# W's six block sums made by GpSimd, A's store issued by SyncE, and W's first scale spread by a matmul

## The chip, the core and the metric

One core of a Trainium2 chip runs the whole program. The metric is the device time of one launch in microseconds, the median of several runs; the profile is of one such execution. Engines are TensorE (PE in the rows, PEld for its weight loads), VectorE (DVE), ScalarE (ACT), GpSimd (POOL) and SyncE (SP, which only issues DMAs here). An engine works through its own instruction stream in order and waits in it on semaphores.

## What is computed

```
x   = x + matmul(fq(layernorm(x), s1, z1), fq(ctx, s2, z2))     # x: 2 x 1024 x 2048, ctx: 2 x 2048 x 2048
out = x + ffn(layernorm(x))
fq(x, s, z) = (clip(round(x/s + z), 0, 255) - z) * s
ffn(x): logits = x @ W_router.T ; top 2 of 8 experts, their softmax weights normalised -> w
        h = x @ lora_A (per expert, rank 16) ; lora = sum over experts of (h * w) @ lora_B, times 2
        return x @ W_base.T + b_base + lora                        # W_base: 2048 x 2048
```

## The kernel before

Phase one is the quantised product. x stands as 16 tiles of 128 rows (t = 0 to 15), ctx as 64 units u of 128 x 1024. Four lists, `SYNC`, `VEC`, `SCA` and `POOL` (lines 220 to 230), give the order of phase one on SyncE, VectorE, ScalarE and GpSimd, written out by hand. Letters with a number are steps. On SyncE: X, A and B load tile t of x (whole, first half, second half), C loads unit u of ctx, T transposes quantised tile t by DMA, P and R spill the two halves of the finished x tile to `x1d` in HBM, Y loads such a tile back for phase two, W loads a block of W. On VectorE: L is the layernorm of tile t, E evacuates group g of PSUM (`evac`, line 901, followed by two statistics instructions). On ScalarE: U quantises tile t to bytes (`xq`), V centres the transposed tile (`xc`), K centres unit u (`cc`). On GpSimd: C quantises unit u (`quantise_ctx`, line 568). TensorE multiplies tile pairs (8, 9), (10, 11) and so on in the third quarter (b = 1, h = 0), with all 16 units of ctx for a pair before the next, and single tiles in the last quarter (b = 1, h = 1), each 32 matmuls.

The LoRA matrix A and the router are split into two fp16 parts `AHI` and `ALO` and stored to `arwd` by `astore` (lines 588 to 591), in the GpSimd list between C41 and C42. Tiles 10 and 11 of x go into memory that `AHI` uses, so that SyncE's `xload` waits for that store (`s_aw`, lines 367 and 368), and all of its list behind it.

Phase two is the feed-forward product. It runs in fp16 with each factor split in two parts (three passes), and by seven block products instead of eight (as Strassen and Winograd do), for two column halves of W. Iterations i = 0 to 7 take the first half of the columns, i = 8 to 15 the second, each with two row tiles of x. The four blocks B11, B12, B21, B22 of W are 128 x 4096 fp32 each, and four sums are made of them: T3 = B22 - B12, T2 = T3 + B11, T1 = B22 - T2, T4 = B21 - T2. `wsum` makes them for the first half, `wsum1` for the second, all on VectorE. Each of the seven operands is then split: ScalarE writes the high part (`whi`, `whi1`), VectorE the low part (`wlo`, `wlo1`), two instructions each. The split needs a scale from the largest absolute row sum of W: `wabs` and `wtotal` sum on ScalarE, `wspread` writes the 128 sums to HBM and reads them back on every partition, `wscale` takes the maximum and derives the scale.

Products P1 to P7 (`product`, line 1358) use B11, B21, T2 (P6), T1 (P5), T3 (P7), B22 (P3) and T4 (P4). Their order is P1, P2, h, P6, P5, P3, P7, P4 at i = 0 and P1, P2, P6, P7, P5, P3, P4 at i = 8. A product waits for the low part of its operand (`s_wl`) and for the read of its bank (`ev`, r1 to r7). At the first iteration of each half the operands are made while the products run; these two places are called the first seam (i = 0, about 295 to 380 us) and the second seam (the end of i = 7 and i = 8, about 694 to 776 us).

Of x, ScalarE makes normalised rows (`norms`) and high parts (`chi`), VectorE low parts (`clo`, 128 x 1024, both inputs in SBUF) and sums (`csum`). `badd` adds the bias (both inputs in SBUF), `blo` is the low part of lora_B (both in SBUF), `ev` has one input in PSUM and one in SBUF.

ScalarE's `whi(3)` (T1) waits until T1 and T4 are both made (lines 730 and 731), and `whi1(5)` (T1 of the second half) does too (lines 743 to 745). `yload` of iteration 9 waits for T2 and for the low part of T3 (lines 414 to 416).

Of the kernel before, what the change touches and what calls it, by code (L numbers as in the profile page):

```python
def build(nc, x, ctxd, sc, wt, ar, bt, bias, x1d, out):
# [27 lines left out]
    with ctx:  # L29
# [137 lines left out]
        s_wm = sem("s_wm")  # L167
        s_t = sem("s_t")
# [43 lines left out]
        def plan(*lines):  # L212
# [17 lines left out]
        POOL = plan("C0-29 F0 C30-31 H0 C32-41 A0 C42-63 P8-15 R8-10 M0 R11-15")  # L230
# [127 lines left out]
        def _(sp):  # L358
# [36 lines left out]

            def qtrans(t):
# [111 lines left out]
            for kind, i in SYNC:  # L508
                {"X": xload, "A": lambda t: xhalf(t, 0), "B": lambda t: xhalf(t, 1), "C": cload, "T": qtrans, "F": fload, "P": spill_a, "R": spill_b, "Y": yload, "W": rload}[kind](i)
# [953 lines left out]
```

## Time and profile before

| | |
|---|---|
| median of 3 runs | 1056.71 us (1055.82 to 1061.08) |
| the profiled execution | 1056.88 us, span 1054.7 us |
| TensorE matmul busy | 919.1 us (87%), 4650 instructions |
| VectorE busy | 654.4 us (62%) |
| ScalarE busy | 383.8 us (36%) |
| GpSimd busy | 149.9 us (14%) |

All times of rows are in microseconds from the start of the span. Between the span and the execution's time lie 2.2 us. A matmul row whose bracket names a wait stands behind an idle stretch of TensorE. In the page's table of slices TensorE's granted clock is full (9 tenths or more) except around 150 to 200 us, at the two seams and in a few slices between, and the DMA engines are nearly full from the start to about 275 us.

### The profile page before, as it was taken

How to read it: one execution, taken by the hardware profiler on the slowest of the kernel's cores; microseconds unless marked ns; L12 is line 12 of the kernel's file. 1: busy time of each engine (PE TensorE's matmuls, PEld its weight loads, DVE VectorE, ACT ScalarE, POOL GpSimd, SP SyncE). 2: the span in 40 equal slices, each digit the busy share in tenths (PEclk: the TensorE clock that was granted, in tenths of full speed). 3: DMA queues.
4: the chain of work that ended last, by engine and by line, in shares of the span. 5: the costliest groups of instructions: out<-in, count | busy, mean ns of one | idle time of the engine just before them, and what ended most of it. 6: DMA issues, size and time to landing. Idle time of an engine off the chain costs nothing. (4 is left out here: it accounts for less than half of the span.)

```text
span 1054.7 us, 12350 instructions
## 1 busy us (share of the span) xinstructions
PE 919.1 (87%) x4650; PEld 431.9 (41%) x4672; DVE 654.4 (62%) x1007; ACT 383.8 (36%) x343; POOL 149.9 (14%) x198
## 2 busy tenths in 40 slices
PE   0989945889946578999899999998799999999997
PEld 0334422334413243545354554543244444444443
DVE  7896778534679866354746546459957545654621
ACT  3363436761534623223332333036332331331300
POOL 2643312242010011101111110100000000000000
PEclk9999987899979788999999999998899999999999
DMA  9998979799566577999799897974479898998831
GB/s 315 299 305 314 378 271 265 228 326 363 160 182 183 111 177 201 207 169 241 174 220 214 202 258 165 217 294 145 95 201 198 222 228 216 174 240 207 165 95 40
DMA packets 294142, 228.50 MB, mean 217 GB/s; under 512 B 248816, under 2 KB 249840, under 8 KB 289856
## 3 DMA queue, kind: packets, MB, share of 16 engines
q1 hardware_dynamic: 283200, 191.05, 71.0%
q0 software_dynamic: 10880, 36.61, 10.5%
q8 instruction: 40, 0.66, 0.3%
q14 instruction: 22, 0.18, 0.1%
HBM read 131.04 MB, written 36.28 MB: 159 GB/s over the span
## 5 line engine op out<-in xcount | busy, mean ns | idle before, releaser
L1380 PE MATMUL PS<-WS,XT 128*128 128x512 f16 x2688 | 602.6, 386 | 56.9 <-DVE OQ L1162 23.0
L1380 PEld LDWEIGHTS PS<-WS,XT 128*128 128x128 f16 x2688 | 265.8, 99 | 387.2 <-issue 57.4
L1334 PE MATMUL PS<-QC,QT 128*128 128x512 bf16 x1002 | 230.9, 390 | 63.9 <-DVE QC L895 29.0
L1162 DVE SCALAR_TENSOR_TENSOR OQ<-PS,ZI,OQ 128x512 f32<-128x512 f32 x128 | 94.2, 747 | 156.5 <-PE PS L1380 78.2
L1334 PEld LDWEIGHTS PS<-QC,QT 128*128 128x128 bf16 x1024 | 101.2, 100 | 193.0 <-issue 64.1
L704 ACT ACTIVATE NX<-Yb 128x1024 f16<-128x1024 f32 x60 | 63.1, 1052 | 117.3 <-DMA XT<-NX 54.4
L1088 DVE TENSOR_TENSOR NX<-Ya,NX 128x1024 f16<-128x1024 f32 x45 | 53.8, 1220 | 83.8 <-ACT NX L704 82.6
L568 POOL TENSOR_SCALAR CU<-CS,K,S 128x1024 uint8<-128x1024 f32 x64 | 79.9, 1250 | 146.5 <-DMA CS<-ctx 129.5
L598 POOL DMA_DIRECT2D out<-OQ x64 | 34.7, 542 | 450.9 <-DVE OQ L1162 440.9
L1088 DVE TENSOR_TENSOR NX<-Yb,NX 128x1024 f16<-128x1024 f32 x60 | 73.1, 1218 | 36.1 <-ACT NX L704 36.0
L672 ACT ACTIVATE QC<-CU,K 128x1024 bf16<-128x1024 uint8 x52 | 58.2, 1141 | 55.6 <-POOL CU L568 54.7
L907 DVE SCALAR_TENSOR_TENSOR XR<-PS,K,XR 128x1024 f32<-128x1024 f32 x32 | 40.8, 1276 | 55.8 <-PE PS L1334 55.8
L704 ACT ACTIVATE NX<-Ya 128x1024 f16<-128x1024 f32 x45 | 45.7, 1044 | 59.6 <-DMA XT<-NX 49.5
L689 ACT ACTIVATE Ya<-Ya,L 128x2048 f32<-128x2048 f32 x15 | 31.4, 2093 | 92.2 <-DMA Ya<-x1d 92.1
L689 ACT ACTIVATE Yb<-Yb,L 128x2048 f32<-128x2048 f32 x15 | 31.4, 2093 | 78.9 <-DMA Yb<-x1d 78.9
L1394 PE MATMUL PS<-BW,HT 128*128 128x512 f16 x192 | 50.0, 399 | 9.2 <-issue 5.9
L1411 PEld LDWEIGHTS PS<-ARW,XT 128*128 128x128 f16 x768 | 46.1, 98 | 1.9
L1411 PE MATMUL PS<-ARW,XT 128*128 128x136 f16 x768 | 46.8, 223 | 0.0
L851 DVE BATCH_NORM_STATS2 ST<-XR 128x6 f32<-128x512 f32 x64 | 39.8, 680 | 8.6 <-DMA XR<-x 8.5
L914 DVE BATCH_NORM_STATS2 ST<-XR 128x6 f32<-128x512 f32 x64 | 41.2, 685 | 1.1
L1079 DVE TENSOR_TENSOR OQ<-OQ,BI 128x512 f32<-128x512 f32 x64 | 41.0, 683 | 0.0
L658 ACT ACTIVATE XU<-XR,LN 128x2048 uint8<-128x2048 f32 x15 | 31.3, 2086 | 24.3 <-DVE LN L864 16.0
(121 smaller groups left out, 482.7 us busy)
## 6 DMA issues: line engine op xcount, KB each, us to landing
CS<-ctx SPq DMA_DIRECT2D x64, 512.0 KB, 6.4
OQ<-x1d SPq DMA_DIRECT2D x64, 256.0 KB, 4.7
out<-OQ POOLq DMA_DIRECT2D x64, 256.0 KB, 6.6
Ya<-x1d SPq DMA_DIRECT2D x15, 1024.0 KB, 6.5
Yb<-x1d SPq DMA_DIRECT2D x15, 1024.0 KB, 8.7
XR<-x SPq DMA_DIRECT2D x9, 1024.0 KB, 7.9
x1d<-XR SPq DMA_DIRECT2D x16, 512.0 KB, 8.0
FB<-wt SPq DMA_DIRECT2D x4, 2048.0 KB, 16.8
```

Source lines behind the costliest of these rows:

```text
L568: pool.tensor_scalar(CU[u % 4][:, :], CS[u % 4][:, :], k(RV2), z2, ALU.mult, ALU.add).then_inc(s_cp, 1)
L672: act.activation(QC[h][:, kt, :], CU[u % 4][:, :], ACT.Identity, bias=k(C2N)).then_inc(s_ks, 1)
L689: act.activation(Y[e][:, :], Y[e][:, :], ACT.Identity, bias=L2[:, 0, t:t + 1], scale=L2[:, 1, t:t + 1]).then_inc(s_nm, 1)
L704: act.activation(NX[nxb(n)][:, 0, :], Y[e][:, h * HF:(h + 1) * HF], ACT.Copy).then_inc(s_hi, 1)
L914: ins = dve.bn_stats(ST2[:, t, 2 * h + q, :], XR[:, h, x_slot(t), q * CH:(q + 1) * CH])
L1079: tt(OQ[b][:, :], OQ[b][:, :], BI[:, o * CH:(o + 1) * CH], ALU.add).then_inc(s_bq, 1)
L1088: tt(NX[nxb(n)][:, 1, :], blkof(e, h), NX[nxb(n)][:, 0, :], ALU.subtract).then_inc(s_lo, 1)
L1162: stt(OQ[ob][:, :], PS[:, bank(i, b), :], ZI[:, half(i), 1:2].bitcast(F32), OQ[ob][:, :], ALU.mult, ALU.add).then_inc(s_rd, 1)
L1334: ins = pe.matmul(PS[:, 2 * (t % 4) + c, :], QT[t][:, kt, :], QC[h][:, kt, c * CH:(c + 1) * CH], start=(kt == 0), stop=(kt == KT - 1))
L1380: ins = pe.matmul(PS[:, bank(i, b), :], XT[SLOT[i, j]][:, xi, kt, :], WS[half(i)][blk][:, :, kt // 2, wi, kt % 2, :], start=(fresh and n = ...
L1394: ins = pe.matmul(PS[:, bank(i, b), :], HT[i % 2][:, e, xi, :], BW[:, o, wi, :], start=False, stop=(n == 2), skip_group_check=(b == "X" or ...
L1411: ins = pe.matmul(PS[:, 7, e * 136:(e + 1) * 136], XT[SLOT[i, j]][:, xi, kt, :], ARW[:, g[wi] + kt, :], start=(n == 0), stop=(n == 47))
```

## The change

A's store moves from the GpSimd list to the SyncE list (Q0), and that list is rearranged around it. Six of the eight sums move from VectorE to GpSimd: T1 and T4 of the first half, T3, T2, T1 and T4 of the second. The four absolute sums of W are made in a row on ScalarE ahead of `chi(0, 2)`; the total is written 128 times in bf16 (`FSB`), and a matmul with an identity matrix inside the last quarter of phase one lays all totals on every partition. T3, T2 and the scale come earlier on VectorE in the first seam.

```diff
-            "P0-1 C32 P2-3 C33 R0 P4-5 C34 R1 P6-7 C35 A8-9 C36-37 B8 C38 B9 C39 R2-3 C40-41 X10-11 C42 A12-13 T8 C43 B12-13",
-            "T9 C44 R4-5 C45 A14-15 T10 C46 B14-15 T11 C47 T12 R6-7 T13 C48-49 T14 C50 T15 C51-63 Y0 W0-3")
+            "P0-1 C32-33 R0 C34 R1 C35 A8-9 C36-37 B8 C38 B9 C39-41 R2-3 Q0 P2-3 C42-43 T8 C44 T9 C45 X10-11 C46-47 R4-5",
+            "P4-5 A12-13 T10 B12-13 T11 P6-7 C48 A14-15 R6-7 T12 B14-15 T13 C49 T14 C50 T15 C51-63 Y0 W0-3")
-            "L8-9 E12-13 L10-13 E14-15 S0 L14-15 E16-23 M1")
+            "L8-9 E12-13 L10-11 E14-15 L12-13 S0 L14-15 E16-23 M1")
-        POOL = plan("C0-29 F0 C30-31 H0 C32-41 A0 C42-63 P8-15 R8-10 M0 R11-15")
+        POOL = plan("C0-29 F0 C30-31 H0 C32-63 P8-15 R8-15")
```

```diff
+            def wsum0(blk):
+
+                f = lambda b, p: FB[b][:, 4 * p:4 * p + 4, :, :].rearrange("p a b c -> p (a b c)")
+                pool.wait_ge(s_t, 2)
+                if blk == T1:
+                    slots_free(pool, 1, 0, 1, 2, 3)
+                    for p in range(2):
+                        ins = pool.tensor_tensor(f(T1, p), f(B22, p), f(T2, p), ALU.subtract)
+                else:
+                    pool.wait_ge(s_wl, 4)
+                    pool.wait_ge(s_wa, 4)
+                    for p in range(2):
+                        ins = pool.tensor_tensor(f(T4, p), f(B21, p), f(T2, p), ALU.subtract)
+                ins.then_inc(s_t, 1)
+
+            def wsum1(blk):
...
+                        ins = pool.tensor_tensor(y, b22[:, 2048 * p:2048 * (p + 1)], y, ALU.subtract)
...
+                        ins = pool.tensor_tensor(xp, y, xp, ALU.add)
...
+                    ins = pool.tensor_tensor(b22, b22, x, ALU.subtract)
...
+                    ins = pool.tensor_tensor(x, b21, x, ALU.subtract)
+                ins.then_inc(s_t, 1)
...
+            wsum0(T1)
+            wsum0(T4)
...
+                if i == NPAIR - 1:
+                    wsum1(T3)
+                    wsum1(T2)
+                store(i, (1, 1), (0, 0), (0, 1))
+                store(i, (1, 0))
+                if i == NPAIR - 1:
+                    wsum1(T1)
+                    wsum1(T4)
```

```diff
-            wabs(0)
+            for n in range(4):
+                wabs(n)
+            wtotal()
             chi(0, 2)
-            wabs(1)
-            wabs(2)
             chi(0, 3)
-            wabs(3)
-            wtotal()
+            whi(0)
             chi(0, 4)
-            whi(0)
             whi(1)
...
+                act.activation(FSB[:, :], FS[:, 8:9].to_broadcast([128, 128]), ACT.Copy).then_inc(s_wb, 1)
...
+            def wspread():
+
+                pe.wait_ge(s_ev, 28)
+                pe.wait_ge(s_wb, 1)
+                pe.matmul(PS[:, 6, 0:128], FSB[:, :], ID[:, :], start=True, stop=True).then_inc(s_wp, 1)
...
+                    if (b, t, kt) == (1, 6, 0):
+                        wspread()
+                    if (b, t, kt) == (1, 7, 0):
+                        pe.wait_ge(s_wq, 1)
```

`wsum0` and `wsum1` stand on GpSimd, `wsum0` behind R15, and wait for what the sums waited for before: in the first half T1 and T4 are two instructions of 128 x 2048 each, in the second T3 and T2 are two each and T1 and T4 one of 128 x 4096 each. `FSB` is written on ScalarE at the end of `wtotal`, and the new `wspread` is TensorE's.

VectorE's order in the first seam becomes: E26, E27, T3, `clo(0, 2)`, S1, S3, E28, T2, `wscale(0)`, E29, `clo(0, 3)`, S2, `wlo(0)`, E30, `clo(0, 4)`, S4C, `wlo(1)`, E31, `clo(0, 5)`, `clo(0, 6)`, `wlo(2)`, r1, `wlo(3)`, where T1 stood ahead of `clo(0, 6)` and T4 ahead of `wlo(3)`. In the second seam the four calls of `wsum1` fall out of VectorE's order and nothing else in it moves. The last quarter's `wspread` reads bank 6 only after E27.

## Rows read from the trace of the kernel before

**Rows 1.** Timeline of TensorE, 140 to 195 us: start, length, idle before and its releaser.
```profile
159.50 1.01 PE L1334 MATMUL PS<-QC,QT 128*128 128x512 bf16 x2 [14.49 <-issue]
165.09 14.36 PE L1334 MATMUL PS<-QC,QT 128*128 128x512 bf16 x53 [4.58 <-ACT QT L662]
...
189.66 10.58 PE L1334 MATMUL PS<-QC,QT 128*128 128x512 bf16 x37 [3.06 <-ACT QC L672]
```

**Rows 2.** Timeline of TensorE at the two seams.
```profile
309.32 7.45 PE L1380 MATMUL PS<-WS,XT 128*128 128x512 f16 x24 [14.60 <-DVE WS L1027]
347.85 12.16 PE L1380 MATMUL PS<-WS,XT 128*128 128x512 f16 x48 [11.33 <-DVE OQ L1162]
...
730.48 17.16 PE L1380 MATMUL PS<-WS,XT 128*128 128x512 f16 x72 [3.21 <-DVE WS L1062]
755.55 13.08 PE L1380 MATMUL PS<-WS,XT 128*128 128x512 f16 x48 [7.91 <-DVE WS L1062]
```

**Rows 3.** Timeline of all engines, 118 to 143 us.
```profile
118.25 1.48 DVE L964 SCALAR_TENSOR_TENSOR ALO<-ARS,SI,AHI 128x1024 f16<-128x1024 f32 x2 [1.22 <-ACT AHI L681]
...
125.31 1.56 SPq L381 DMA_DIRECT2D CS<-ctx  x2
...
126.47 2.47 DVE L851 BATCH_NORM_STATS2 ST<-XR 128x6 f32<-128x512 f32 x4 [1.72 <-DMA XR<-x]
...
132.14 0.22 DVE L864 SCALAR_TENSOR_TENSOR LN<-LN,S 128x1 f32<-128x1 f32 x1
...
137.72 0.54 POOL L591 DMA_DIRECT2D arwd<-ALO x1
...
138.28 2.08 ACT L658 ACTIVATE XU<-XR,LN 128x2048 uint8<-128x2048 f32 x1
...
142.86 1.24 SPq L369 DMA_DIRECT2D XR<-x  x2
```

**Rows 4.** Instructions grouped by line and form: count, busy, mean ns of one.
```profile
L568 POOL TENSOR_SCALAR CU<-CS,K,S 128x1024 uint8<-128x1024 f32 x64 | 79.9, 1250 | 146.5 <-DMA CS<-ctx 129.5 <-ACT QC L672 12.3 <-DVE QC L895 3.6
L1088 DVE TENSOR_TENSOR NX<-Yb,NX 128x1024 f16<-128x1024 f32 x60 | 73.1, 1218 | 36.1 <-ACT NX L704 36.0
L1039 DVE TENSOR_TENSOR FY<-FX,FY 128x2048 f32<-128x2048 f32 x2 | 4.5, 2288 | 2.8 <-DMA FX<-wt 2.8
```

**Rows 5.** Timeline of VectorE and GpSimd, 129 to 132 us.
```profile
129.91 0.16 DVE L862 SCALAR_TENSOR_TENSOR LN<-LN 128x1 f32<-128x1 f32 x1
130.21 1.20 POOL L568 TENSOR_SCALAR CU<-CS,K,S 128x1024 uint8<-128x1024 f32 x1 [1.24 <-ACT QC L672]
130.35 1.05 DVE L862 SCALAR_TENSOR_TENSOR LN<-LN 128x1 f32<-128x1 f32 x1
```

**Rows 6.** Timeline of the first seam, 300 to 340 us.
```profile
300.57 0.28 DVE L1013 TENSOR_REDUCE FX<-WG 128x1 f32<-128x128 f32 x1 [3.54 <-DMA WG<-wmd]
...
317.86 1.28 DVE L907 SCALAR_TENSOR_TENSOR XR<-PS,K,XR 128x1024 f32<-128x1024 f32 x1
...
331.02 4.41 DVE L1004 TENSOR_TENSOR FT<-FB,FT 128x4096 f32<-128x4096 f32 x1
...
335.53 3.90 ACT L732 ACTIVATE WS<-FT,ZI 128x2048 f16<-128x2048 f32 x2 [15.72 <-DVE FT L1004]
```

**Rows 7.** Timeline of the second seam, 694 to 753 us.
```profile
694.12 3.90 ACT L750 ACTIVATE WS<-FX,ZI 128x2048 f16<-128x2048 f32 x2 [14.54 <-PE PS L1380]
...
697.58 4.49 DVE L1039 TENSOR_TENSOR FY<-FX,FY 128x2048 f32<-128x2048 f32 x2 [2.79 <-DMA FX<-wt]
...
716.91 0.33 SPq L424 DMA_DIRECT2D Ya<-x1d  x1
...
725.73 4.60 DVE L1062 SCALAR_TENSOR_TENSOR WS<-FX,ZI,WS 128x2048 f16<-128x2048 f32 x2
...
730.97 3.88 ACT L750 ACTIVATE WS<-FX,ZI 128x2048 f16<-128x2048 f32 x2
...
739.79 4.42 DVE L1050 TENSOR_TENSOR FX<-FX,FX 128x4096 f32<-128x4096 f32 x1
```

More of the change, by code:

```diff
@@ L118, in build @@
         RI = small("RI", [128, 2, 8], U32)
+        ID = small("ID", [128, 128], BF16)
+        IDI = at("IDI", [128, 128], I32, R4 + 36 * KB)
         HWF = at("HWF", [128, 2, 8, 16], F32, LN_AT)
-        WG = [at("WG0", [128, 128], F32, LN_AT), at("WG1", [128, 128], F32, RB[1] + 8 * KB)]
+        FSB = at("FSB", [128, 128], BF16, LN_AT)
+        WG = at("WG", [128, 128], F32, RB[1] + 8 * KB)
         PS = ctx.enter_context(nc.psum_tensor("PS", [128, 8, CH], F32))
@@ L167, in build @@
         s_wm = sem("s_wm")
+        s_wb = sem("s_wb")
+        s_wp = sem("s_wp")
+        s_wq = sem("s_wq")
         s_t = sem("s_t")
@@ L394, in fload, with astore @@
                 sp.dma_start(BS[:, :], bt).then_inc(s_lb, 16)
+            def astore(_):
+                sp.wait_ge(s_al, 5)
+                sp.dma_start(arwd[:, 0:24, :], AHI[:, :, :]).then_inc(s_aw, 16)
+                sp.dma_start(arwd[:, 24:48, :], ALO[:, :, :]).then_inc(s_aw, 16)
             def qtrans(t):
@@ new lines, in wsum1 @@
+            def wsum1(blk):
+                x = FX1[B11][:, :, :, :].rearrange("p a b c -> p (a b c)")
+                b22, b21 = (FX1[b][:, :, :, :].rearrange("p a b c -> p (a b c)") for b in (B22, B21))
+                if blk == T3:
+                    pool.wait_ge(s_wr[0], 48)
+                    pool.wait_ge(s_wr[2], 32)
+                    for p in range(2):
+                        y = FY1[p][:, :, :, :].rearrange("p a b c -> p (a b c)")
+                        ins = pool.tensor_tensor(y, b22[:, 2048 * p:2048 * (p + 1)], y, ALU.subtract)
+                elif blk == T2:
+                    pool.wait_ge(s_t, sum1(T3))
+                    pool.wait_ge(s_wl, low1(B11, 1))
+                    for p in range(2):
+                        y = FY1[p][:, :, :, :].rearrange("p a b c -> p (a b c)")
+                        xp = x[:, 2048 * p:2048 * (p + 1)]
+                        ins = pool.tensor_tensor(xp, y, xp, ALU.add)
+                elif blk == T1:
+                    pool.wait_ge(s_t, sum1(T2))
+                    pool.wait_ge(s_wl, low1(B22, 1))
+                    ins = pool.tensor_tensor(b22, b22, x, ALU.subtract)
+                else:
+                    pool.wait_ge(s_t, sum1(T1))
+                    pool.wait_ge(s_wl, low1(T2, 1))
+                    pool.wait_ge(s_wr[3], 32)
+                    ins = pool.tensor_tensor(x, b21, x, ALU.subtract)
+                ins.then_inc(s_t, 1)
@@ L633, in _ @@
                     pool.wait_ge(s_rx, 1)
-                    wspread(1)
-                store(i, (1, 1), (0, 0), (0, 1), (1, 0))
+                    wspread()
[7 more added lines that the diff above has]
+                    wsum1(T4)
         @block.scalar
@@ L1170, in _ @@
             dve.tensor_copy(IO[:, :], IOI[:, :])
+            ts(ID[:, :], IDI[:, :], 0.0, None, ALU.is_equal)
             for kind, i in VEC:
@@ L1178, in _ @@
             evac(27)
+            wsum(T3)
             clo(0, 2)
@@ L1181, in _ @@
             csum(0, S3)
-            wsum(T3)
             evac(28)
+            wsum(T2)
+            wscale(0)
+            evac(29)
             clo(0, 3)
             csum(0, S2)
-            wsum(T2)
-            evac(29)
+            wlo(0)
+            evac(30)
             clo(0, 4)
             csum(0, S4C)
-            wscale(0)
-            wlo(0)
-            evac(30)
-            clo(0, 5)
             wlo(1)
             evac(31)
-            wsum(T1)
+            clo(0, 5)
             clo(0, 6)
@@ L1199, in _ @@
             ev(0, "r1")
-            wsum(T4)
             wlo(3)
```

74 lines of the change are left out of this document (18 added, 56 removed).

## The prediction

> **What bounds the kernel now.** I read the page's slices first: TensorE is busy 87% of the span, and its busy digit drops at the start, around 150 to 200 us and at the two seams. Then I read TensorE's own timeline for its gaps, since between them it runs matmul on matmul and only a gap can be won or lost. Around the third quarter of phase one it stands 14.5, 4.6 and 3.1 us, and once more between [rows 1]. In the first seam its two longest gaps are 14.6 us ahead of P1 and 11.3 us ahead of P5; in the second it stands 3.2 us ahead of P2 and 7.9 us ahead of P5 of iteration 8 [rows 2]. Last I followed each gap back through the other engines. After the second seam the chain that ended last is almost all matmuls, so what a seam loses is in the end time one for one.
>
> **Phase one: the store of A.** The cause of the 14.5 us is in SyncE's queue. It issues C41 by 126.9 and then nothing until 142.86, where tiles 10 and 11 wait for A's store. Both parts of A are ready at 119.7, but GpSimd issues the store's second half only at 137.7, behind C41 [rows 3]. Queued behind that wait are C42, T8, T9 and all later loads of x, and TensorE waits for them. In the change the store stands in SyncE's list behind C41 and R3, so it should go out by 127, and 4 spills of 0.5 MB each (P4 to P7) no longer stand ahead of these loads. What is late next? The layernorm of tile 8 starts at 126.5 now, waiting for x; its load comes earlier, but VectorE evacuates E10 and E11 first, so about 124.8, and 5.9 us for its steps (126.5 to 132.4 now) gives 130.7. ScalarE quantises tile 8 by 132.9 where it did so from 138.3 to 140.4 [rows 3]. T8 is then issued at 133, not 146. But tiles 10 and 11 now stand behind T8, C44, T9 and C45, and T9 waits for the quantising of tile 9 (139.5), so they are issued at about 141.6, only 1 us earlier than before. Their layernorms end at 153 and 159. From there ScalarE's order (U10 K44 U11 V10 K45 V11 U12 K46 U13 V12 K47) is a chain with a transposing DMA (about 6 us) at T10, T11 and T12, and with B12-13 issued only behind T10: I get U12 at 172, V12 at 180 and K47 at 181, where TensorE now gets K47 at 189.7 [rows 1]. I take 8 us of gain for phase one. The bounds are 1 us (all of it is lost to loads that now come later) and 14 us (the first gap gone and nothing behind it late). The third and fourth quarter run without long gaps, so the gain is passed on; the loads of W move with it, since they wait for the spills of x.
>
> **First seam.** Now the scale comes by two DMAs through HBM and VectorE reads it at 300.6 [rows 6]; P1 starts at 309.3 [rows 2]. By the matmul, with all four absolute sums made in a row, it should be known 10 us earlier, and P1 start at about 300. The matmul itself costs TensorE under 0.5 us, and the wait for the maximum ahead of tile 7 up to 1 us; both are hidden, as TensorE then waits for `wlo(0)` anyway. This gain isn't passed on, because P5 waits for T4. ScalarE's `whi(3)` waits for T1 and T4, and `wlo(3)`, `norms(1)`, `chi(1, 0)`, `clo(1, 1)` and r2 follow in a row until P5 at 347.85 [rows 2, 6]. Now T4 ends at 335.4, on VectorE [rows 6]. In the change GpSimd may start T1 only after R15, so after E31, which moves from 317.9 [rows 6] to about 309.6; that is 311.5 with the spill's issue. What a sum costs on GpSimd no row shows. The lower bound for 128 x 2048 is 2.4 us, twice its one-input instruction on 1024 columns (1.20 to 1.25 us) [rows 4, 5]; the upper is 4.8 us, if each of the two inputs takes that long. I take 4.6, twice VectorE's 2.29 for the same shape [rows 4], near the upper bound, for the next paragraph's reason. A whole sum is then 9.2 us, where VectorE takes 4.4 [rows 7].
>
> **The port.** VectorE's one-column instruction L862 takes 0.16 us; the one that began at 130.35, just behind a GpSimd instruction of 130.21 to 131.41, took 1.05 and ended with it [rows 5]. Its two inputs lie in SBUF. So an instruction of VectorE with two SBUF inputs stands until GpSimd's has ended. If the two share one read path, GpSimd can draw only one input at a time, hence twice the time for two. The low parts, `clo`, `csum`, `badd` and `blo` all have two SBUF inputs; `ev` and the evacuation have one in PSUM.
>
> The Trainium skill says the same (SBUF — State Buffer, section "Who interferes with whom"): a VectorE instruction with two SBUF inputs and a GpSimd instruction that reads SBUF exclude each other for the whole instruction. It also gives (GPSIMD Engine Reference, section "Performance versus the Vector engine") 4497 ns for this instruction on 2048 columns; no run so far shows it, and with it the sum below would be 1 us less. The rule speaks against this change: work taken from VectorE still holds it up.
>
> So in the first seam: T1's first half 311.5 to 316.1; VectorE's two `clo` (2.4) and `wlo(2)` (4.6) to 323.1; three halves of 4.6 to 336.9. T4 ends 1.5 us later than before, P5 1.3 us later: +1. Bounds: -8 (GpSimd at 2.4 per half) and +3.
>
> **Second seam.** Here VectorE loses 17.8 us of work (four sums of 4.4 to 4.5 [rows 7]), and that gains nothing, since the sums are a chain. Step by step, in the clock of the kernel before:
> - `whi1(0)`'s parts are ready at 696.1 and 698.0 [rows 7], so `wlo1(0)` takes VectorE from 696.1 to 700.8; T3, whose data lands at 697.5, waits for it on GpSimd: 700.8 to 710.0 instead of 697.6 to 702.1.
> - T2's first half 710.1 to 714.7; `wlo1(1)` (T3) stands behind it, 714.7 to 719.3; T2's second half to 723.9; three `badd` stand behind that, to 725.8; r6 and r7 to 727.2; `wlo1(2)` to 731.8; r5; `wlo1(3)` to 737.1. It ended at 730.3 [rows 7], so P2 is 6.8 us late.
> - The loads of Ya and Yb (716.9 now [rows 7]) wait for T2: 724.0. ScalarE's `norms` and `chi` end at 738.1, and `whi1(4)` starts then, where it started at 731.0 [rows 7]. `wlo1(4)` ends at 744.7, two `clo` at 747.1.
> - T1 747.1 to 756.2; `blo` 1.3; T4 757.5 to 766.6 (now both are done from 739.8 [rows 7] to 748.7).
> - `whi1(5)` and `wlo1(5)` take 6.8 us from there as they do now (748.7 to 755.5 [rows 2, 7]): P5 at 773.4 instead of 755.55, +18 us.
>
> Bounds: with GpSimd at 2.4 us per half the same steps give P5 at 756.0, so +0.5 is the lower end; at 4.8 per half they give 775.5, +20. A gain needs sums as short as VectorE's own, so I exclude one beyond 2 us. TensorE's gap ahead of L22 at i = 7 vanishes, but P5 is later than it.
>
> **Sum.** -8 + 1 + 18 = +11 us on the profiled execution's 1056.88: 1067.9. That execution is 0.2 us above the median, so 1068. Moving the store of A and spreading the scale cost nothing elsewhere; the identity matrix is made at the start, under the first load of x.
>
> **Rivals.**
> - *No lock for long instructions* (or one that VectorE always wins at once). For it: the row of the lock is of 1.2 us instructions only. Against: it held VectorE to the end of that one. Then the second seam has T3 to 706.7, T2 to 715.9, T1 and T4 737.7 to 756.1, `wlo1(5)` to 762.9: +7. In the first, T4 ends at 329.9 and P5 5 us earlier. Sum: -8 - 5 + 7 = -6, 1051: the faster side. It decides if a low part that overlaps a sum still takes 2.35 us. Chance 0.14.
> - *GpSimd is quick*, 2.4 us per half: -8 - 8 + 0.5 = -15.5, 1041. For it: its one-input rate is close to VectorE's. Against: the shared path. Chance 0.06.
> - *Phase one gives back nothing*: B12-13, A14-15 and B14-15 are behind T10, T11 and T12, and DMA is nearly full there; or the absolute sums come too late for the matmul ahead of tile 6 and TensorE stands on it. Then -1 + 1 + 18 (up to +20): 1075. Chance 0.12.
> - *A larger gain in phase one, or a milder alternation at the port*, with the mechanism as forecast: -12 + 0 + 13, about 1058. Chance 0.13.
> - The forecast: 0.55.
>
> **How the numbers follow.** The forecast's own range is 1062 to 1074. The range wanted takes in the rival without the lock and the one without the gain, and leaves out the quick GpSimd and the worst end: 1050 to 1076. About 0.5% (5 us) is what a measurement of this kernel can tell from no change. Slower by more: the forecast and phase one's rival, 0.67, less some of the forecast's low end, 0.64. Within: 0.16. Faster: 0.20.
>
> **What would show it.** Right: SyncE without its gap at 127 to 143; T8 issued near 133; TensorE's pair (8, 9) done about 8 us earlier; the first seam's P1 about 17 us earlier and its P5 about 7; GpSimd sums of 4.5 to 4.8 us per 2048 columns, more where they waited; low parts of VectorE that overlap them well over 2.35 us; a gap of 15 us or more ahead of P5 of iteration 8. Wrong: `wlo1(1)` at its old length beside T2; T1 and T4 of the second half in under 12 us together; or a gap on TensorE at tile 6 of the last quarter.

## The result, and the profile after

| | before | after |
|---|---|---|
| median, 4 runs each on one chip | 1056.26 us (1051.03 to 1061.08) | 1068.24 us (1063.56 to 1073.57) |
| ratio of the two, 95% interval | | 1.011 (1.0062 to 1.0157) |
| the profiled execution, its span | 1056.88 us, 1054.7 us | 1070.97 us, 1069.2 us |
| TensorE matmul busy | 919.1 us | 920.6 us |
| VectorE busy | 654.4 us | 667.5 us |
| GpSimd busy | 149.9 us | 207.0 us |

The change makes the kernel slower, by 12 us in the medians and 14.1 us between the two profiled executions. The total forecast, 1068.0, is met; its three terms are not all met, and this section and the experiments take them one by one. Some executions ran at a lower granted clock and took longer; among the medians of this document that moves only e1's by more than 0.5 us, since one of its four is such a one (1095.49 us at a clock of 0.904), and it is left out there.

The first thing to see in the page is that VectorE lost six sums of 4.4 us, 27 us of work, and is busy 13 us more, so its other instructions are 40 us longer. The rows of VectorE grouped by form show where most of that sits (line, operation, count, busy time, mean ns of one). The two forms of `clo` differ only in the tile they read, and both took 1.2 us before ([rows 4] has the Yb form). Of after:

```profile
L1110 DVE TENSOR_TENSOR NX<-Ya,NX 128x1024 f16<-128x1024 f32 x45 | 79.8, 1799 | 74.6 <-ACT NX L758 72.6
L1110 DVE TENSOR_TENSOR NX<-Yb,NX 128x1024 f16<-128x1024 f32 x60 | 73.1, 1219 | 40.2 <-ACT NX L758 40.1
```

A mean of 1799 ns over 45 is not 45 slower instructions. It is 43 of 1.2 us and two very long ones, of 18.6 and 9.9 us, which the seams below show. Busy time here contains waiting.

**Phase one, third quarter.** TensorE's gaps (start, length, idle before and its releaser), to set against [rows 1]:

```profile
163.49 1.04 PE L1351 MATMUL PS<-QC,QT 128*128 128x512 bf16 x4 [2.85 <-ACT QC L726]
173.24 1.89 PE L1351 MATMUL PS<-QC,QT 128*128 128x512 bf16 x4 [8.71 <-ACT QC L726]
179.90 1.89 PE L1351 MATMUL PS<-QC,QT 128*128 128x512 bf16 x4 [4.78 <-ACT QC L726]
191.26 4.02 PE L1351 MATMUL PS<-QC,QT 128*128 128x512 bf16 x9 [9.47 <-ACT QC L726]
```

The gap of 14.5 us at 159.5 is gone, and in the place of it and of the smaller ones behind it (4.6, 5.3 and 3.1 us) stand four of 2.9, 8.7, 4.8 and 9.5 us, all behind a centring on ScalarE. TensorE gets K47 at 191.3, where it got it at 189.7. The last quarter starts at 239.3 (237.8 before). The first term, a gain of 8 us, was a loss of 1.5.

**First seam**, TensorE, to set against [rows 2]:

```profile
290.65 8.77 PE L1351 MATMUL PS<-QC,QT 128*128 128x512 bf16 x31 [3.00 <-DVE FX L1059]
301.67 7.03 PE L1403 MATMUL PS<-WS,XT 128*128 128x512 f16 x24 [2.26 <-DVE WS L1077]
311.19 7.03 PE L1403 MATMUL PS<-WS,XT 128*128 128x512 f16 x24 [2.50 <-DVE WS L1077]
...
338.44 7.68 PE L1403 MATMUL PS<-WS,XT 128*128 128x512 f16 x24 [14.54 <-DVE OQ L1184]
349.28 5.96 PE L1403 MATMUL PS<-WS,XT 128*128 128x512 f16 x19 [3.16 <-DVE OQ L1184]
```

P1 starts 7.6 us earlier (301.67), P6 7.3 us later (338.44), P5 1.4 us later (349.28). What stands between is VectorE and GpSimd in the same stretch:

```profile
313.08 8.99 POOL L632 TENSOR_TENSOR FT<-FB,FT 128x2048 f32<-128x2048 f32 x2
313.48 18.58 DVE L1110 TENSOR_TENSOR NX<-Ya,NX 128x1024 f16<-128x1024 f32 x1
322.02 8.95 POOL L637 TENSOR_TENSOR FT<-FB,FT 128x2048 f32<-128x2048 f32 x2
331.98 1.21 DVE L1110 TENSOR_TENSOR NX<-Yb,NX 128x1024 f16<-128x1024 f32 x1
333.12 4.61 DVE L1077 SCALAR_TENSOR_TENSOR WS<-FT,ZI,WS 128x2048 f16<-128x2048 f32 x2
```

T1 and T4 are four instructions of 4.5 us without a pause, and one `clo` of VectorE, 1.2 us of work, is open from 313.5 to 332.1, through all four. The next `clo`, `wlo(2)` and the read r1, for which P6 waits, stand behind it.

**Second seam**, to set against [rows 7] and the last two of [rows 2]:

```profile
697.25 4.61 DVE L1084 SCALAR_TENSOR_TENSOR WS<-FX,ZI,WS 128x2048 f16<-128x2048 f32 x2 [1.37 <-ACT WS L807]
699.63 11.08 POOL L649 TENSOR_TENSOR FY<-FX,FY 128x2048 f32<-128x2048 f32 x2 [4.71 <-DMA FX<-wt]
...
712.78 11.21 DVE L1084 SCALAR_TENSOR_TENSOR WS<-FY,ZI,WS 128x2048 f16<-128x2048 f32 x2 [6.54 <-ACT WS L807]
...
737.63 18.11 PE L1403 MATMUL PS<-WS,XT 128*128 128x512 f16 x72 [14.05 <-DVE WS L1084]
...
743.67 11.01 DVE L1110 TENSOR_TENSOR NX<-Ya,NX 128x1024 f16<-128x1024 f32 x2
743.90 9.69 POOL L660 TENSOR_TENSOR FX<-FX,FX 128x4096 f32<-128x4096 f32 x1 [10.10 <-DVE WS L1084]
753.67 9.67 POOL L665 TENSOR_TENSOR FX<-FX,FX 128x4096 f32<-128x4096 f32 x1
755.26 9.16 DVE L1089 SCALAR_TENSOR_TENSOR BW<-BRAW,ZI,BW 128x1024 f16<-128x1024 f32 x1
763.43 3.89 ACT L807 ACTIVATE WS<-FX,ZI 128x2048 f16<-128x2048 f32 x2 [21.39 <-POOL FX L665]
...
770.22 5.10 PE L1403 MATMUL PS<-WS,XT 128*128 128x512 f16 x16 [14.48 <-DVE WS L1084]
```

P2 starts at 737.6 (730.5 before) and P5 at 770.2 (755.6), and the span ends 14.5 us later. P5 is 14.7 us late, of which 1.1 was there before the seam (h of iteration 7 starts at 673.7, before at 672.6): the seam costs 13.6. Here the two engines take turns. The rows of single lines (shortest, median and longest in ns, first and last start) show T2's halves and those of `wlo1(1)`:

```profile
L656 POOL TENSOR_TENSOR FX<-FY,FX x2: 4531/5549/6567, 710.8 to 715.3; 128x2048 f32<-128x2048 f32 x2
L1084 DVE SCALAR_TENSOR_TENSOR WS<-FY,ZI,WS x2: 4690/5646/6601, 712.8 to 717.4; 128x2048 f16<-128x2048 f32 x2
```

T2's first half runs from 710.8 to 715.3, and the first half of `wlo1(1)`, begun at 712.8, ends 2.2 us behind it, at 717.5. T2's second half, begun at 715.3, takes 6.6 us, 2.1 more than its own 4.5, and VectorE's second half in turn ends 2.2 us behind that. T1 and T4 of this seam are single instructions of 9.7 us; T1 began 1.0 us before the first `clo` ended, and the second `clo`, open from 744.8 to 754.7, ended 1.1 us behind T1. So each of the two sums waits about 1 us for a `clo` and takes some 8.7 us by itself; that is worked out, as no whole sum on GpSimd ran without such a turn in it.

### The profile page after: what moved, and what is told of

It is laid out like the page before. It is cut to its first block and busy times, and to the rows that moved or that the text cites. A ratio compares the mean times of both kernels' runs of the same rounds, so it can differ in the third digit from the quotient of the medians.

```text
span 1069.2 us, 12358 instructions
## 1 busy us (share of the span) xinstructions
PE 920.6 (86%) x4651; PEld 431.7 (40%) x4673; DVE 667.5 (62%) x1000; ACT 384.8 (36%) x344; POOL 207.0 (19%) x205
## 5 line engine op out<-in xcount | busy, mean ns | idle before, releaser
L1110 DVE TENSOR_TENSOR NX<-Ya,NX 128x1024 f16<-128x1024 f32 x45 | 79.8, 1799 | 74.6 <-ACT NX L758 72.6
## 6 DMA issues: line engine op xcount, KB each, us to landing
FB<-wt SPq DMA_DIRECT2D x4, 2048.0 KB, 17.5
```

Source lines behind the costliest of these rows:

```text
L1110: tt(NX[nxb(n)][:, 1, :], blkof(e, h), NX[nxb(n)][:, 0, :], ALU.subtract).then_inc(s_lo, 1)
```

## Experiments

For all of them the first number is the median, beside that of the kernel before on the same chip (1055.45 for e1 to e4, 1055.56 for e5 to e8, 1054.49 for e9 and e10), with the ratio and its 95% interval (the ratio on record, which is not exactly the quotient of the two medians). One table holds what the profiles say of the seams. "h to P5" is from the start of h at i = 7 to P5 at i = 8, so it contains the second seam and nothing that came earlier; "between" is from h at i = 1 to h at i = 7, where no experiment changed anything. Each row of it is one profiled execution.

| kernel | P1 | P5, first seam | between | h to P5 |
|---|---|---|---|---|
| before | 309.3 | 347.9 | 282.0 | 82.9 |
| after | 301.7 | 349.3 | 283.3 | 96.5 |
| e1, sums alone | 308.4 | 353.0 | 277.7 | 96.3 |
| e2, sums back | 301.3 | 342.0 | 281.1 | 81.8 |
| e3, store alone | 304.7 | 343.3 | 287.2 | 82.1 |
| e4, S0 and T12 moved | 304.0 | 351.7 | 281.2 | 96.2 |
| e5, T3 and T2 alone on GpSimd | 299.6 | 347.1 | 283.3 | 88.5 |
| e6, T1 and T4 alone on GpSimd | 301.1 | 348.8 | 279.6 | 91.2 |
| e7, other instructions | 299.8 | 330.8 | 281.2 | 86.4 |
| e8, the best parts | 294.9 | 335.3 | 280.0 | 82.2 |
| e9, low part ahead | 299.7 | 351.7 | 276.5 | 96.9 |
| e10, sums with pauses | 301.0 | 346.9 | 279.2 | 96.6 |

**e1: the kernel before, with the six sums on GpSimd and nothing else.**

```diff
 (vector, first seam)
-            wsum(T1)
             clo(0, 6)
             wlo(2)
             ev(0, "r1")
-            wsum(T4)
             wlo(3)
 (vector, second seam)
-                    wsum1(T3)
-                    wsum1(T2)
-                    wsum1(T1)
-                    wsum1(T4)
 (gpsimd, in the places of the changed kernel)
+            wsum0(T1)
+            wsum0(T4)
+                    wsum1(T3)
+                    wsum1(T2)
+                    wsum1(T1)
+                    wsum1(T4)
```

> The kernel before with only the six sums moved to GpSimd, all else as before. Theory (a sum takes GpSimd about 4.5 us per 2048 columns, and GpSimd and a VectorE instruction with two SBUF inputs exclude each other): P2 of iteration 8 about 6 us late, P5 of iteration 8 13 to 15 us late, and 0 to 3 us in the first seam, together 14 to 17 us: 1070 to 1074. Rival, that the loss comes from the rearranged first phase and not from the sums: within 3 us of the kernel before.

Measured 1072.96 us, 1.0214 (1.0148 to 1.028). The sums alone cost 17.5 us by the medians and 22.6 by the ratio, more than the whole change, so that its other parts should bring a gain (e2). P5 is 5.1 us later in the first seam (0 to 3 expected), and h to P5 is 96.3, as in the kernel after (96.5) and 13.4 over the kernel before (13 to 15 expected): 18.5 us for the two seams.

**e2: the changed kernel, with the six sums back on VectorE.**

```diff
 (vector, first seam)
             clo(0, 5)
+            wsum(T1)
             clo(0, 6)
             wlo(2)
             ev(0, "r1")
+            wsum(T4)
             wlo(3)
 (gpsimd)
-            wsum0(T1)
-            wsum0(T4)
 (second seam: T3, T2, T1, T4 likewise, in their old places)
```

> The changed kernel with its six sums back on VectorE in their old places. Theory: the second seam is as in the kernel before (gaps of about 3 and 8 us), the first seam keeps the earlier P1 (about 302) and now hands it on, P5 at 341 to 343 instead of 347.9: 1049 to 1053, 4 to 7 us under the kernel before. Rival, that the matmul for the scale and the wait on TensorE cost what they bring: 1056 to 1059.

Measured 1047.69 us, 0.9939 (0.9904 to 0.9974), 20.5 us under the kernel after and 8 us under the kernel before. The store's new list, the absolute sums in a row and the matmul together are worth 8 us, and it comes from the scale, at P1. In phase one nothing is gained:

```profile
239.71 5.52 PE L1389 MATMUL PS<-QC,QT 128*128 128x512 bf16 x17 [3.86 <-DVE XR L956]
...
301.25 7.03 PE L1441 MATMUL PS<-WS,XT 128*128 128x512 f16 x24 [3.94 <-DVE WS L1081]
```

The last quarter starts at 239.7 (237.8 before), and P1 at 301.3 (309.3). P5 is at 342.0, 7.3 us ahead of the kernel after, and h to P5 14.7 us shorter. These two, 22.0 us, are what the sums cost; the profiled executions differ by 23.9, the medians by 20.5.

**e3: the kernel before, with A's store on SyncE behind C41 and no other step moved.**

```diff
-... C40-41 X10-11 C42 A12-13 T8 ...
+... C40-41 Q0 X10-11 C42 A12-13 T8 ...
-            ... H0 C32-41 A0 C42-63 ...
+            ... H0 C32-63 ...
```

> The kernel before with only the store of A issued by SyncE, between C41 and X10-11, the lists otherwise as before. If SyncE's wait for that store (127 to 143 us) is what sets TensorE's gaps from 145 to 190, tiles 10 and 11 are asked for at about 135 to 138 and all behind them follows: pair (8, 9) ends 4 to 7 us earlier than 190.7, and the time is 1050 to 1053. Rival, that DMA is the limit there in any order: pair (8, 9) ends within 2 us of 190.7 and the time is that of the kernel before.

Measured 1054.53 us, 0.9996 (0.9965 to 1.0027): no change, where 1050 to 1053 were expected. The profile says why so little of the gap was to be had. SyncE's queue:

```profile
127.32 0.46 SPq L398 DMA_DIRECT2D arwd<-AHI  x1
127.82 0.47 SPq L399 DMA_DIRECT2D arwd<-ALO  x1
140.15 1.24 SPq L369 DMA_DIRECT2D XR<-x  x2
```

The store's second half goes out 9.9 us earlier than before (127.8, not 137.7), and the loads behind it 2.7 us earlier (140.15, not 142.86; 135 to 138 expected). Before, it landed 5.1 us after its issue; here it takes 12.3. In this kernel the DMA engines are busy for the whole stretch from 127 to 137 us (share 1.03 and 1.02 in its two halves); in the kernel before their share had fallen to 0.42 from 132 to 137, just ahead of the store. So most of SyncE's gap was never GpSimd's lateness but the time that the loads, spills and store already asked for take to land. The store also changed its queue, from GpSimd's to SyncE's, where it stands behind those transfers; how much of the 12.3 us that makes no run separates. TensorE gets K47 3 us earlier (186.8; 4 to 7 expected for the end of the pair). Its gap at 159.5 shrinks from 14.5 to 11.4 us, the last quarter starts 3.5 us earlier (234.3), P1 and P5 of the first seam are 4.6 us earlier. The end of this execution is not, since "between" took 287.2 us in it, 5.2 more than in the kernel before. In the twelve kernels of the table "between" runs from 276.5 to 287.2 with no pattern that follows their edits, so it looks like a spread from execution to execution, though with one trace of each kernel that is not shown. The ratio's interval leaves room for a gain of 0.35%, 3.7 us, at most: the 4.6 us do not all arrive at the end, and why is open.

**e4: the changed kernel, with S0 behind L14-15 on VectorE, and T12 ahead of A14-15 and R6-7 on SyncE.**

```diff
-... L10-11 E14-15 L12-13 S0 L14-15 E16-23 M1
+... L10-11 E14-15 L12-13 L14-15 S0 E16-23 M1
-... T11 P6-7 C48 A14-15 R6-7 T12 B14-15 T13 ...
+... T11 P6-7 C48 T12 A14-15 R6-7 B14-15 T13 ...
```

> The changed kernel with two steps moved in phase one: the statistics of phase two (S0) behind the layernorms of tiles 14 and 15 on VectorE, and T12 ahead of the loads A14-15 and the spills R6-7 on SyncE. If the late quantising of tile 13 (behind S0) and the late landing of T12 held K47 back in the changed kernel, K47 ends at 186 to 188 instead of 191.2 and the time falls by 3 to 4 us to about 1065. Rival, that the loads of x alone hold it: no change from 1068.

Measured 1073.51 us, 1.0186 (1.0127 to 1.0245), no gain over the kernel after (1068.24), where 1065 was expected. The local step came, and more of it than the 3 to 5 us expected, and what came next took more than it gave:

```profile
184.51 15.84 PE L1351 MATMUL PS<-QC,QT 128*128 128x512 bf16 x63 [4.91 <-ACT QC L726]
...
205.37 1.27 DVE L962 SCALAR_TENSOR_TENSOR XR<-PS,K,XR 128x1024 f32<-128x1024 f32 x1
...
206.69 1.03 PE L1351 MATMUL PS<-QC,QT 128*128 128x512 bf16 x2 [5.48 <-DVE XR L962]
```

K47 is ready at 184.5, not 191.3, and TensorE then stands 5.5 and 1.5 us on the evacuation E16, which now waits in VectorE's order for L14, L15 and S0. The last quarter starts at 241.7, later than in the kernel after (239.3). Where the order is written by hand, one step taken from a chain is a step put ahead of another.

**e5 and e6: the changed kernel with half of the second seam's sums back on VectorE.** In e5 T1 and T4 go back, in e6 T3 and T2.

```diff
 e5 (vector)
                     clo(q, 0)
                     clo(q, 1)
+                    wsum1(T1)
+                    wsum1(T4)
 e5 (gpsimd)
-                    wsum1(T1)
-                    wsum1(T4)
```

> The changed kernel with T1 and T4 of the second half back on VectorE; T3 and T2 of that half and the first half's two sums stay on GpSimd. Theory (slow and exclusive): the low part of T3 still stands beside T2, P2 of iteration 8 keeps its gap of about 14 us (6 us more than it would be late on VectorE), P5's gap falls from 14.5 to about 8; from h of iteration 7 to P5 of iteration 8 it takes 88 us, where all sums on VectorE gave 82 and all on GpSimd 96.5. Time about 1060. Rival (slow, but VectorE isn't held): T2's longer time lies beside the low part of T3 and P2 comes as with all sums on VectorE: 82 to 83 us.

> The changed kernel with T3 and T2 of the second half back on VectorE; T1 and T4 of that half and the first half's two sums stay on GpSimd. P2's gap falls back to about 3 us, T1 and T4 take 19.4 us in a row instead of 8.9, less 2.4 us of the two clo that no longer stand ahead of them: P5 8 us late, 90 us from h of iteration 7 to P5 of iteration 8. Time about 1062. The rival without the lock expects the same here, 90 to 92, since the chain is GpSimd's own; only if GpSimd were slow because VectorE holds it would this be under 86.

Measured 1058.73 us, 1.0032 (1.0004 to 1.0061), for e5 and 1063.46 us, 1.0066 (1.0036 to 1.0096), for e6. h to P5 is 88.5 in e5 and 91.2 in e6, over the 81.8 of e2: 6.7 us for T3 and T2, 9.4 us for T1 and T4, together 16.1 where both moved cost 14.7. So neither pair alone is the cause, and the rival by which VectorE isn't held (82 to 83 in e5) is out. Both kernels moved as expected (88 and 90). VectorE and TensorE in e5:

```profile
711.43 11.22 DVE L1109 SCALAR_TENSOR_TENSOR WS<-FY,ZI,WS 128x2048 f16<-128x2048 f32 x2 [6.53 <-ACT WS L804]
...
736.28 18.15 PE L1430 MATMUL PS<-WS,XT 128*128 128x512 f16 x72 [14.04 <-DVE WS L1109]
760.90 12.61 PE L1430 MATMUL PS<-WS,XT 128*128 128x512 f16 x48 [6.47 <-DVE WS L1109]
```

The 4.6 us of `wlo1(1)` took 11.2, as in the kernel after, and P5 then waits 6.5 us, about as in the kernel before (7.9). From the end of `wlo1(4)` to P5 e6 takes 26.5 us (736.2 to 762.7) and e5 17.9 (743.0 to 760.9). The 8.6 us between them are, to 0.3 us, the sums' length, 19.4 us on GpSimd with their turns in them against 8.8 on VectorE (two of 4.4, as [rows 7]), less 2.3 us for two `clo` that stand ahead of T1 on VectorE and beside it on GpSimd.

**e7: what holds the port.** The changed kernel, with the two sums of the first seam as writes without an input, and T3 and T2 of the second as instructions with one input. It leaves these four sums out, so its time is no gain; it is there for its trace.

```diff
-                        ins = pool.tensor_tensor(f(T1, p), f(B22, p), f(T2, p), ALU.subtract)
+                        ins = pool.memset(f(T1, p), 0.0)
-                        ins = pool.tensor_tensor(f(T4, p), f(B21, p), f(T2, p), ALU.subtract)
+                        ins = pool.memset(f(T4, p), 0.0)
-                        ins = pool.tensor_tensor(y, b22[...], y, ALU.subtract)
+                        ins = pool.tensor_scalar(y, b22[...], 1.0, 0.0, ALU.mult, ALU.add)
-                        ins = pool.tensor_tensor(xp, y, xp, ALU.add)
+                        ins = pool.tensor_scalar(xp, y, 1.0, 0.0, ALU.mult, ALU.add)
```

> The changed kernel with other instructions in the place of four sums on GpSimd, so that these sums are left out: T1 and T4 of the first half are memsets of the same size (they write and read nothing), T3 and T2 of the second half are one-input instructions (times 1 plus 0) of the same size. Theory (the reads exclude each other): clo(0, 5), 18.6 us in the changed kernel, takes its 1.2 us beside the memsets; the low part of T3 is still stretched by the one-input instruction beside it, though by 2.4 us at a time and not 4.5; and the one-input instruction takes 2.4 us for 2048 columns where the sum took 4.5. Rival (any GpSimd instruction excludes): clo(0, 5) is stretched beside the memsets too.

One execution, 1042.34 us. First seam, then second:

```profile
311.14 3.56 POOL L632 MEMSET FT<- 128x2048 f32 x2
311.56 1.21 DVE L1110 TENSOR_TENSOR NX<-Ya,NX 128x1024 f16<-128x1024 f32 x1
312.68 1.22 DVE L1110 TENSOR_TENSOR NX<-Yb,NX 128x1024 f16<-128x1024 f32 x1
313.82 4.61 DVE L1077 SCALAR_TENSOR_TENSOR WS<-FT,ZI,WS 128x2048 f16<-128x2048 f32 x2
...
686.45 3.76 POOL L656 TENSOR_SCALAR FX<-FY 128x2048 f32<-128x2048 f32 x2
688.44 6.17 DVE L1084 SCALAR_TENSOR_TENSOR WS<-FY,ZI,WS 128x2048 f16<-128x2048 f32 x2 [1.31 <-ACT WS L807]
```

Beside a GpSimd instruction that only writes, `clo` takes 1.21 us and `wlo(2)` 4.61, their lengths of old. Beside one that reads, VectorE is held again: the first half of `wlo1(1)`, started at 688.44, stood until T2's replacement had ended at 690.2 and ended 2.1 us later, at 692.35, so that the pair took 6.17 us and not 4.6. So it is GpSimd's reads that VectorE waits for, as far as one execution shows it. The one-input instruction takes 1.9 us per 2048 columns (3.76 for two; 2.4 expected), the two-input sum 4.5 in the other kernels. TensorE's gaps fall with them: P5 of the first seam is at 330.8, and h to P5 is 86.4, the rest being T1 and T4, which stayed.

**e8: the parts that brought a gain, together.** The sums on VectorE, the scale by the matmul, the store on SyncE, and otherwise the two lists of the kernel before.

```diff
 (against e2)
-            "P0-1 C32-33 R0 C34 R1 C35 A8-9 ... C39-41 R2-3 Q0 P2-3 C42-43 T8 C44 T9 C45 X10-11 C46-47 R4-5",
+            "P0-1 C32 P2-3 C33 R0 P4-5 C34 R1 P6-7 ... R2-3 C40-41 Q0 X10-11 C42 A12-13 T8 C43 B12-13",
-... L10-11 E14-15 L12-13 S0 ...
+... L10-13 E14-15 S0 ...
```

> All sums on VectorE, the scale by the matmul, the store of A issued by SyncE, and the lists of phase one as in the kernel before but for that store. If phase one's rearranged lists cost about 4 us against the old lists with the store moved (pair (8, 9) done at 187.7 and at 191.5), and this is handed on, the time is 1043 to 1045, under the 1047.7 of the kernel with the sums back. Rival: the stretch between the seams gives it back, 1047 to 1049.

Measured 1042.89 us, 0.9901 (0.9861 to 0.9941): 1% faster than the kernel before and 25 us faster than the one after.

TensorE's first gap of the third quarter is 11.6 us and it gets K47 at 186.3 us, much as in e3 (11.4 and 186.8), 4.3 us before e2; P1 is 6.4 us earlier than in e2, and the medians of e2 and e8 lie 4.8 us apart. So the old lists with the store moved are better than the rearranged ones, as expected. The times alone don't show it, since e3 could not be told from no change and the intervals of e2 and e8 overlap a little; with the profiles' readings of K47 and P1 it is likely.

**e9 and e10: who gets the port.** Both are the changed kernel. e9 puts the low part ahead of the two `clo`; e10 has GpSimd wait between the four sums of the first seam.

```diff
 e9 (vector)
+            wlo(2)
             clo(0, 5)
             clo(0, 6)
-            wlo(2)
 e10 (gpsimd; T4 likewise)
                         ins = pool.tensor_tensor(f(T1, p), f(B22, p), f(T2, p), ALU.subtract)
+                        if p == 0:
+                            ins.then_inc(s_gg, 1)
+                            pool.wait_ge(s_gg, 1)
...
+                    pool.wait_ge(s_t, 3)
```

> The changed kernel with wlo(2) ahead of clo(0, 5) and clo(0, 6) on VectorE; nothing else moves. In the first seam one clo stood 18.6 us through four consecutive sums of GpSimd, while in the second seam each half of wlo1(1) got the port at the end of one sum (2.3 us of its own after at most 4.4 us of waiting). Theory one: it is the kind of VectorE's instruction; the low part, with a scalar and two inputs, gets its turn between two sums where clo does not. Then the first half of wlo(2) starts at about 313.5, takes under 7 us, T1's second half is stretched to about 6.6 us, and P6 starts about 12 us earlier than 338.4. Rival: it is GpSimd's side, four sums handed over without a pause; then the first half of wlo(2) is open for about 19.7 us, to 1 to 2 us behind the end of T4, and P6 starts within 3 us of where it did.

> The changed kernel with GpSimd made to wait between the four sums of the first seam: each starts only when the semaphore of the one before has come. The wait by itself costs under 0.2 us each. Theory: VectorE gets the port where GpSimd pauses, as between T1 and T4 of the second half, where T4 waits for T1's semaphore and a clo ran for 1.1 us between them. Then clo(0, 5) ends 1.1 us behind T1's first half (about 5.2 us in all, not 18.6), T1's second half is stretched to about 5.5 us, clo(0, 6) and the two halves of wlo(2) each follow at the end of one more sum, P6 starts 6 to 10 us earlier, and T4 ends 4 to 6 us later. Rival: a pause of 0.1 us makes no difference; clo(0, 5) is open for 18 us or more again and P6 starts near 338.4.

One execution each, 1068.57 and 1066.27 us. VectorE in e9, and VectorE and GpSimd in e10:

```profile
311.48 19.65 DVE L1077 SCALAR_TENSOR_TENSOR WS<-FT,ZI,WS 128x2048 f16<-128x2048 f32 x1
```

```profile
312.37 9.98 POOL L633 TENSOR_TENSOR FT<-FB,FT 128x2048 f32<-128x2048 f32 x2
312.76 5.21 DVE L1118 TENSOR_TENSOR NX<-Ya,NX 128x1024 f16<-128x1024 f32 x1
317.90 5.54 DVE L1118 TENSOR_TENSOR NX<-Yb,NX 128x1024 f16<-128x1024 f32 x1
...
322.52 11.78 POOL L642 TENSOR_TENSOR FT<-FB,FT 128x2048 f32<-128x2048 f32 x2 [0.17 <-POOL FT L633]
323.37 13.08 DVE L1085 SCALAR_TENSOR_TENSOR WS<-FT,ZI,WS 128x2048 f16<-128x2048 f32 x2
```

(In e10 T4 also waits for T1's semaphore, `s_t` at 3, which it doesn't in the changed kernel.) In e9 the low part stands 19.65 us for its 2.3, as the rival had it: the kind of VectorE's instruction isn't what decides. In e10 `clo` is done after 5.21 us, as the theory had it, and the engines take turns from there on. That buys little, as every turn lengthens the sums: they end at 334.3, not 331.0, though they start 0.7 us earlier, the halves of `wlo(2)` take 6.6 us each, and P6 comes at 337.2 (I had 6 to 10 us earlier than 338.4), P5 at 346.9, where P2 is 0.7 us earlier too.

## Why the prediction came out as it did

The total was right, 1068.0 against 1068.24, because two errors of it cancel in part, and luck covers the rest: a gain of 8 us that did not come, and a loss set 5.5 us too high. Between the two profiled executions the sum reads: phase one +1.5, first seam -0.1 (P5 is 1.4 us late and the last quarter had been 1.5), second seam +13.6. These are 15.0; the end of the span is 14.5 us later, as 0.3 us come back between P5 and h of iteration 7 and 0.2 behind the second seam. Against the steps' -8, +1 and +18 the misses are +9.5, -1.1 and -4.4, together +4. The profiled execution is 3 us over the forecast's 1067.9, and it lies 2.7 us above its kernel's median, which is why the median agrees to less than a microsecond. That closeness is luck.

- **Phase one, -8: wrong.** The first steps held: SyncE's gap is gone, the store's halves go out at 124.9 and 126.2, tile 8 is quantised from 132.5 on and T8 issued at 134.6 (forecast 133). The step that failed is "tiles 10 and 11 are issued at about 141.6".

```profile
129.35 2.26 SPq L387 DMA_DIRECT2D CS<-ctx  x2
...
141.13 2.45 POOL L580 TENSOR_SCALAR CU<-CS,K,S 128x1024 uint8<-128x1024 f32 x2 [9.89 <-DMA CS<-ctx]
142.36 1.15 ACT L726 ACTIVATE QC<-CU,K 128x1024 bf16<-128x1024 uint8 x1 [7.79 <-POOL CU L580]
143.41 2.08 ACT L712 ACTIVATE XU<-XR,LN 128x2048 uint8<-128x2048 f32 x1
...
145.57 1.24 SPq L414 DMA_TRANSPOSE XV<-XU  x1
...
147.47 1.24 SPq L375 DMA_DIRECT2D XR<-x  x2
```

  GpSimd waits 9.9 us for C42, which was issued at 129.4 and is there only at 141.1, with the store and the spills issued just ahead of it; that these slowed it is argued from the order, not shown. ScalarE centres it (K42) ahead of U9 in its order, so tile 9 is quantised from 143.4 on and not from 137.5, T9 goes out at 145.6 (139.5 forecast), and X10-11 behind it at 147.5: 5.9 us later than forecast and 4.6 later than before. I had counted the DMAs' issues and let the landings stand as they were. The forecast also took SyncE's wait for the cause of TensorE's gap without asking how much of it was landing; e3 shows 12.3 us of it with the store issued at once.
- **The end of phase one.** A second step was left out: the last steps of L13 come behind S0 in VectorE's stream. The statistics of tile 13 end at 179.0, its aggregation follows at 183.6, and U13 starts at 186.2. K47 comes last, behind V12 and T12, which is issued at 178.9 behind the loads of A14-15 and lands at 187.1. V12 stands behind U13 in ScalarE's order and starts at 188.2 (180 forecast); U12, which stands ahead of both, started at 176.7 (172 forecast). e4 moves S0 and T12 and K47 comes 6.7 us earlier: shown for the two together, not for each. That this is no gain for the kernel, since E16 then waits, is shown too.

```profile
179.05 1.12 DVE L1025 BATCH_NORM_AGGREGATE MV<-ST 128x2 f32<-128x24 f32 x8
...
183.61 0.26 DVE L912 BATCH_NORM_AGGREGATE LN<-ST 128x2 f32<-128x24 f32 x1
```

  The rival "phase one gives back nothing" had the outcome right here. Of its causes, full DMA engines fit (their share is 0.96 to 1.15 from 124 to 141 us) but aren't shown to be the cause, and the gap on TensorE ahead of tile 6 did not come.
- **First seam, +1: right in size, wrong inside.** With the 1.5 us of phase one taken off, P1 starts at 300.2 (forecast 300) and T1 at 311.6 (311.5). The matmul cost TensorE 0.2 us. The wait for the maximum ahead of tile 7 was 3.0 us (forecast up to 1; 0.5 in e2), hidden as said, since P1 starts within 0.5 us of e2's. A half of a sum took 4.50 us, not 4.6. The step that failed is the order at the port: two `clo` and `wlo(2)` were to slip in behind T1's first half, and did not. So T4 ends at 329.5 on that clock, 7.4 us before the forecast, and `wlo(2)` starts at 331.6, 13 us behind it, and the two nearly cancel at P5 (347.8, forecast 349.1). The way to P5 is another than the forecast's too: it had T4's end, then ScalarE's `whi(3)`; in the trace `whi(3)` starts 4.5 us after T4's end, behind the first half of `wlo(2)`, and VectorE's queue follows T4's end without a gap, `clo`, `wlo(2)`, r1 and `wlo(3)`, from 332.0 to 342.9. The forecast costed the shared port by the length of the sums and not by which of the two engines is let through. What the sums cost here, 5.1 us in e1 and 7.3 against e2, is paid out of the scale's gain.
- **Second seam, +18: right in its mechanism, mis-sized by 4.4.** With 1.1 us taken off, `wlo1(0)` starts at 696.2 (forecast 696.1), T3 ends at 709.6 (710.0), the loads of Ya and Yb go out at 723.0 (724.0), and P2 is 6.0 us late (6.8). Engines took turns by halves of `wlo1(1)`, where I had both halves in one turn; `wlo1(4)` ends 2.0 us before the forecast by then. The rest, 2.3 us, is in T1 and T4: from the end of `wlo1(4)` to T4's end 21.9 us were forecast, two `clo`, a sum of 9.1, `blo` of 1.3 and a sum of 9.1. Measured were 19.6: one `clo`, 8.7, one `clo`, 8.7, with `blo` behind. So the term mis-sized is a whole sum, 8.7 for 9.1, and `blo` was not in the chain.
- **The rivals.** No lock for long instructions: wrong, `wlo1(1)` took 11.2 us and `clo` 18.6. Quick GpSimd: wrong, 4.5 us per half. The one with a milder alternation at the port had the two seams at 0 and 13, nearly as measured (-0.1 and 13.6), but phase one at -12.
- **The signs.** SyncE's gap, the length of the sums and the stretched low parts came as forecast. The pair (8, 9) was to be done 8 us earlier, P1 of the first seam 17 and P5 of it 7: K47 came 1.6 us later, P1 7.6 earlier, P5 1.4 later. So the signs told what the total hid.

The forecast had read from [rows 5] that VectorE stands until a GpSimd instruction ends, and the Trainium skill says this of a VectorE instruction with two SBUF inputs and a GpSimd instruction that reads (SBUF — State Buffer, section "Who interferes with whom"): the one that issues first has the shared port for its whole instruction. The trace agrees for single instructions: T3's first half, begun at 699.6, took 6.6 us where the second took 4.5, as the second half of `wlo1(0)`, begun at 699.5, held the port until 701.9. The same section says that a GpSimd instruction which only writes is no hindrance; e7 agrees, with 1.21 us for `clo` beside it. But `clo` of the first seam stood beyond the end of the first sum, through three more, for 18.6 us in all; who comes next at the end of an instruction was my guess, an alternation, and not a reading of a row.

**What stays open.** In the first seam VectorE got no turn in four sums without a pause, in every kernel that has them there (18.58 to 18.60 us), and the pause of e10 gave it one. But the halves of T2 in the second seam have no pause between them either, and there VectorE was let through at 715.3; so it was in e1 between the halves of T3, at 704.1. So the pause was enough in e10's one execution, and is not needed everywhere; what tells the places apart was not found. The kind of VectorE's instruction doesn't, by e9. Three differences remain that no run separates: four sums stand in a row in the first seam and two in the second; the sums of the second write over one of their inputs and those of the first don't; and VectorE asks 0.4 us after the first sum's start in the first seam, 2.0 us after T2's and 0.8 after T3's in e1. Nor is the spread of the stretch between the seams explained, nor where the 4.6 us of e3 go.

## What to carry to other kernels

An engine's work is not off the critical path because another engine does it: ask whether the two share a port, and then add the other engine's work to the first one's waits, for a whole run of instructions and not for one. When an issue is late, see how long the transfer took to land before you count its lateness as the gain; here 10 us of earlier issue gave 2.7 us. And when a forecast of several terms meets its total, check the terms: here the sums alone cost about 20 us (17.5 in e1, 20.5 from e2 to the kernel after) and hid a version 1% faster than the start.

## What the runs showed of the hardware

- One VectorE instruction of 1.2 us with both inputs in SBUF stood 18.6 us beside four consecutive GpSimd sums of 4.5 us (five kernels). With a pause between the sums it stood 5.2 us (one execution). Elsewhere VectorE got its turn between two sums without a pause: the first half of `wlo1(1)` took 4.7 us beside T2.
- GpSimd's two-input sum takes 4.5 us per 128 x 2048 fp32 and 9.7 us per 128 x 4096 with a turn of VectorE's in it, about 8.7 without (worked out), twice what VectorE takes (2.29 and 4.42). A one-input instruction took 1.9 us per 2048 columns, 2.6 us less than the sum, and writing them alone took 1.8 us (e7, one execution).
- A GpSimd instruction that only writes did not hold VectorE (one execution).
- Two stores of 816 KB took 3.7 and 5.1 us to land when GpSimd issued them at 137 us, with the DMA engines' share at 0.42 just before, and 10.1 and 12.3 us when SyncE issued them 10 us earlier among spills and loads, with the share at 1.0. Which part the queue has in that no run separates.
